# Issuing four of an image's eight key-spreading transfers from ACT instead of SP

## The reference

```python
x = x + windowed_attention(group_norm(x))         # 16 heads of 32, windows of 8 x 8, shifted
t = to_tokens(x)                                  # 256 tokens an image
h = layer_norm(t)
q, k, v = split(h @ w_qkv + b_qkv)                # 8 heads of 16
t = t + softmax(q @ k.T * scale) @ v @ w_out + b_out      # "second attention"
h = layer_norm(t)
logits = h @ router_w.T + router_b                # 8 experts, each token goes to its best 2
y = sum over 2 experts of weight * expert(h)      # silu(h1) * h2, then a second product
t = t + y
```

## Time and profile before

| | us |
|---|---|
| median of 3 runs | 778.26 |
| lowest, highest | 772.68, 778.88 |
| the profiled execution | 770.44 |
| its span from first to last instruction | 768.6 |
| share of the span that engines are busy | PE 84%, DVE 67%, ACT 66%, POOL 63% |
| mean granted clock of PE, share of full | 0.952 |

### The profile page before, as it was taken

One profiled execution on the slowest core, in us unless ns is written; L12 is line 12 of the kernel. 1 busy time (PEld: TensorE's weight loads), 2 busy tenths in 40 slices (PEclk: granted clock), 3 DMA queues, 4 the chain that ended last, 5 costly groups with the idle time before them and its releaser, 6 DMA issues. The chain is left out here.

```text
span 768.6 us, 20244 instructions
## 1 busy us (share of the span) xinstructions
PE 643.4 (84%) x7046; PEld 543.4 (71%) x7046; DVE 518.1 (67%) x1513; ACT 503.8 (66%) x1427; POOL 485.9 (63%) x556
## 2 busy tenths in 40 slices
PE   3887989999989899898998989888776699999910
PEld 2766878777778777787777878776564688888800
DVE  4666767888788878878878788884453456566524
ACT  3555788878778777888778887765551166666600
POOL 6354656665767786687867867675465436666645
PEclk9799999999999999999999999999997799999965
DMA  7102013031331303313032230312462213333246
GB/s 198 34 3 35 6 32 70 30 99 20 88 77 41 102 24 93 68 54 102 23 92 48 77 101 23 92 41 77 125 213 92 67 51 93 87 85 93 74 160 195
DMA packets 48074, 59.27 MB, mean 77 GB/s; under 512 B 10370, under 2 KB 41218, under 8 KB 47458
## 3 DMA queue, kind: packets, MB, share of 16 engines
q1 hardware_dynamic: 41846, 45.65, 22.5%
q0 software_dynamic: 4544, 9.38, 3.6%
q10 hardware_dynamic: 1584, 2.95, 1.0%
HBM read 36.00 MB, written 28.64 MB: 84 GB/s over the span
## 5 line engine op out<-in xcount | busy, mean ns | idle before, releaser
L587 POOL TENSOR_TENSOR pb<-pb,rcb 128x512 f32<-128x512 f32 x128 | 156.5, 1223 | 149.8 <-DVE rcb L873 148.5
L628 POOL DMA_INDIRECT ysl<-yo,dst x78 | 75.5, 968 | 58.4 <-DVE yo L1147 42.4
L739 ACT ACTIVATE pb<-pSB,mxb 128x256 f32<-128x256 f32 x128 | 59.5, 469 | 47.2 <-DVE mxb L973 46.6
L739 ACT ACTIVATE pb<-pSA,mxb 128x256 f32<-128x256 f32 x128 | 59.6, 475 | 41.2 <-DVE mxb L973 41.2
L1266 PE MATMUL pTB<-ident,pb 128*128 128x128 f32 x512 | 80.2, 280 | 7.2 <-ACT ptb L753 7.1
L595 POOL TENSOR_TENSOR pa<-pa,rca 128x512 f32<-128x512 f32 x64 | 67.2, 1050 | 28.5 <-DVE rca L1038 28.5
L753 ACT ACTIVATE ptb<-pTB 128x512 f32<-128x512 f32 x128 | 77.1, 602 | 2.0 <-PE pTB L1266 2.0
L523 POOL DMA_INDIRECT slots<-rec,slot x64 | 65.3, 1020 | 15.5 <-issue 14.1
L1266 PEld LDWEIGHTS pTB<-ident,pb 128*128 128x128 f32 x512 | 57.9, 142 | 11.1 <-issue 7.8
L759 ACT ACTIVATE pta<-pTA 128x512 f32<-128x512 f32 x64 | 38.6, 603 | 40.3 <-PE pTA L1358 40.1
L973 DVE TENSOR_REDUCE mxb<-pSB 128x2 f32<-128x512 f32 x64 | 43.9, 686 | 21.1 <-PE pSB L1235 21.0
(11 more groups left out here) (221 smaller groups left out, 1996.5 us busy)
## 6 DMA issues: line engine op xcount, KB each, us to landing
slots<-sel_dram SPq DMA_DIRECT2D x16, 1040.0 KB
kbd<-kst SPq DMA_DIRECT2D x128, 64.0 KB, 2.4
xt<-slots SPq DMA_DIRECT2D x39, 130.0 KB, 2.2
xch<-x_ch_dram SPq DMA_DIRECT2D x4, 512.0 KB, 7.1
xt<-x_tok_dram SPq DMA_DIRECT2D x16, 128.0 KB, 2.4
xch<-t SPq DMA_DIRECT2D x16, 128.0 KB, 2.1
fw<-f_dram SPq DMA_DIRECT2D x1, 2048.0 KB
yc<-ysl SPq DMA_DIRECT2D x8, 256.0 KB, 7.4
```

The source lines that it names most:

```text
L587: pool.tensor_tensor(pb[:, b, :, :], pb[:, b, :, :], rcb[:, b, :].unsqueeze(2).to_broadcast([128, 2, TOK]), ALU.mult).then_inc(sb_nrm, 1)
L628: pool.indirect_dma_start(ysl, bass.IndirectOffsetOnAxis(ap=dst[:, t % YB, n:n + 1], axis=0), yo[:, t % YB, n, :], None).then_inc(y_dma[t ...
L739: last = a.activation(pb[:, b, qc, :], (pSB, pSA)[n % 2][:, qc * TOK:(qc + 1) * TOK], ACT.Exp, bias=mxb[:, b, qc:qc + 1], accum_out=smb[:, ...
```

## The change

SP issues the key transfers of heads 0 to 3 only. ACT issues those of heads 4 to 7, at step 7 of the same iteration, right behind the two evictions of the queries (L710) and ahead of `t2f`. Both wait for `m_klo`, and the same semaphore counts all eight. What is moved, its bytes, its layout and all waits of PE are the same.

```diff
                     wait(sp, m_klo, M.j + 1)
                     if M.j < 2:
                         sp.wait_ge(z_k1, M.j + 1)
-                    for h in range(8):
+                    for h in range(4):
                         rows = slice(D1 * h, D1 * h + D1)
                         sp.dma_start(kbd1[M.par][rows, :, :, h % 4, :].bitcast(f32), kst1[rows, :, :, :].bitcast(f32))\
                           .then_inc(k1_dma[M.par], 16)
...
                         last.then_inc(m_qhi, 1)
+                        a.wait_ge(m_klo, M.j + 1)
+                        if M.j < 2:
+                            a.wait_ge(z_k1, M.j + 1)
+                        for h in range(4, 8):
+                            rows = slice(D1 * h, D1 * h + D1)
+                            a.dma_start(kbd1[M.par][rows, :, :, h % 4, :].bitcast(f32), kst1[rows, :, :, :].bitcast(f32))\
+                             .then_inc(k1_dma[M.par], 16)
```

## The result

The changed kernel takes 863.0 us (median of 4 runs, 861.34 to 866.76), the kernel before 776.3 in the same comparison: a ratio of 1.113 (95% interval 1.106 to 1.119). The forecast was 827 with a range of 795 to 850. The direction was right, the size was not: +87 us where I had +53. The profiled execution has a span of 861.8 us against 768.6 and a mean granted clock of 0.898 against 0.952.

A forecast was written before the change was run, and what follows sets the result against it. PE, busy 84% of the span in a stiff loop, was taken to bound the kernel. 13 images x 4.0 us plus 1 gave 53 us, so 823.4 or 831.3 by baseline; forecast the middle, 827 us, range 795 to 850.

The forecast's parts named there:

- SP loses four issues: SP's issue list: four key issues take 2.54 us instead of 5.08; SP is off the path, but the zeros go out earlier.
- ACT gains four issues: ACT ahead of `t2f`: four issues take 2.54 us, `t2f` starts 2.25 us late, PE's first scores move by 1.7 us.
- Rival A: Only ACT's stall costs, the zeros hold no keys: 13 x 1.7 + 1 = 23 us, say 798 us; chance 0.17.
- The zeros go ahead of ACT's keys: ACT's last keys land behind the zeros, so PE's first scores start 4.0 us later, bounds 1.7 and about 6.
- Behind the first scores: PE after the first scores, images 2 to 14: the 4.0 us delay passes in full, 13 x 4.0 = 52 us.
- rival C: PE's clock falls as well behind two gaps of about 2.3 us: 5.5 us an image, say 847 us; chance 0.13.
- The ends: Images without zeros beside their keys: images 0 and 1 together +1 us; image 15 taken as 0, bounds -1 and +4.
- Rival B: Zeros and ACT's keys take turns piece by piece: scores 2.3 us later an image, period 34.6, say 805 us; chance 0.13.

The follow-up runs named there:

- e1: The changed kernel, but SP waits until all eight key transfers have landed before it issues the zeros; 787.2 us, ratio 1.014.
- e6: The kernel before, with the zeros issued between the fourth and fifth key transfers and 21 filler products instead of 3; 836.9 us, ratio 1.089.
- e3: The changed kernel with 18 filler products instead of 3 ahead of the first scores; 854.9 us, ratio 1.101.
- e10: The changed kernel with ACT's four issues moved behind `t2f` and 21 filler products instead of 3; 843.4 us, ratio 1.100.
- e9: The changed kernel with the zeros written in two issues of 4 KB pieces instead of one of 33 KB pieces; 825.7 us, ratio 1.075.
- e7: The changed kernel with the second half of the zeros issued only after all eight key transfers have landed; 806.1 us, ratio 1.054.
- e2: The kernel before, all keys on SP, with the zeros issued between the fourth and fifth key transfers; 870.3 us, ratio 1.121.
- e4: The kernel before with the key transfers of heads 4 to 7 left out and PE waiting for four; 766.9 us, ratio 0.989.

## Why the prediction was right or wrong

**SP loses four issues: right.** The row of four is 2.53 us long (2.54 said), and the zeros follow 3.21 us behind the first (3.2).

**ACT gains four issues: half right.** Each issue takes 0.61 to 0.83 us, within my bounds or just above. But the earlier trace rows, where a table load stood behind an issue, was the wrong row for evictions: ACT's issues begin while evictions of its list are still running, and the stall is 1.42 us, not 2.25. PE waits 1.6 (e1) to 1.8 us (changed) for `t2f` on average, and 1.0 of it reaches the product of the values (6.17 us behind the first key issue instead of 5.19); I had 1.7. Where only this part acts, as in e1, it costs 0.5 to 0.6 us an image and not 1.7. Rival A by itself was thus much too dear (798 against e1's 787).

**The zeros go ahead of ACT's keys: the right mechanism, its term too small.** I took the scores to start 4.0 us later; they start 4.94 later (12.47 − 7.53). The working put the end of the zeros 7.1 us behind their issue and let the last 128 KB of keys follow at 100 GB/s: 8.35 us. On average the scores began 9.2 us behind the zeros' issue, in the image shown, the worst, 10.7. What was too small is the 7.1. It had been read from windows that book bytes at their start; the last rise of the zeros' semaphore comes 8.0 us behind their issue before, where few keys are in flight beside them, and 8.7 us after (8.0 to 10.2). The keys behind them add less than the 1.25 us that I had, some 0.5. The earlier trace rows had shown a longer hold, a scatter that landed 10.6 us behind the later of two zeros' issues. The bound of about 6, which I had from that row, is as far above the 4.94 as the 4.0 is below it. One reason for rival A, a DMA share of 0.65 or less, was misread too: the earlier trace rows have 0.67, and with keys and zeros in flight together the share is 1.02 from 440 to 442.

**Behind the first scores: wrong.** The step "I let the 4.0 us pass in full" had only the gap. What stands between the first scores and the next image's first key issue grew too, from 24.89 to 26.65 us, 1.8 us an image. That is the clock, rival C's mechanism, which I held for a case of 0.13 beside the forecast. It isn't beside it: gaps of the forecast's own size bring it on. In image 2 of the changed kernel PE waits 2.03 us for `t2f` and 2.10 us for the keys, where I had 2.3 and 2 to 2.5, and the clock is 0.50 from 130 to 132 and 0.53 from 136 to 138. The earlier trace rows had shown a clock of 0.58 behind a stretch with 1.5 us of gaps in four; I had expected gaps of 2.3 us and left the clock at full. e6 measures its price at 2.1 us, where I had estimated 1.5. With fillers in the gap the changed kernel too comes back to 25.1 us between the first scores and the next key issue (e3, e10).

Together: 4.94 + 1.76 = 6.7 us an image where I had 4.0. The thirteen periods behind images 2 to 14 grew by 83.8 us in the traces (73.7 + 10.1) where I had 52, so these two steps lack 32 of the 34 us by which the medians exceed the sum of 53. Rival C, at 5.5 us, 37.8 and 847 us, was the nearest of the cases.

**The ends: wrong by little.** Images 0 and 1 gave −2.4 us and not +1. Of these, 1.0 us stood already before the first key was issued (62.52 against 63.53) and is not the change's. The other 1.4 us goes with the clock as much as with the keys: nothing waits for `t2f` there and PE's wait of 1.13 us for the keys is gone, but the first scores of image 0 start 8.10 us behind the first key issue instead of 7.30, and the clock, at half from 74 to 80 before, is at half from 68 to about 71 only. Image 15 cost 3.8 us, where I took 0 with +4 as a bound: its last keys stand behind the weights as others do behind the zeros. These two nearly cancel. The 8 us at the end of the span, among the experts, belong to no step.

**Rival B and its rule.** Cut into small pieces the zeros hold less, and the keys land ahead of the zeros' end (e9): in that the traces speak for turns between the queues. That three of ACT's four transfers count 3.2 to 3.3 us does not, since they were issued ahead of the zeros or within 0.3 us of them; with no zeros near, in e1, ACT's take 2.4 to 3.6. With the zeros in 33 KB pieces the last of the four takes up to 9.7 us, the keys land with the zeros' end, and the period was 39.1, not B's 34.6. The Trainium skill (DMA: Bandwidth & Descriptors, section on queues, rings and completion order) says that an engine drains a whole packet of several descriptors before it switches to another queue. I had weighed that as if a turn were one piece. No run here shows what a packet holds; e9, with 1.8 us less hold for pieces an eighth of the size, and e7, with a hold that follows the amount, are compatible with long turns and don't prove them.

## What to carry to other kernels

Moving transfers to a second engine's queue saves issue time and gives up the order that one queue had: before it is done, look at what the shortened queue issues next, and whether that is large. Where a large transfer has slack and small ones have a reader waiting, keep it behind them, by the order in one queue or by a wait for their landing. And gaps on PE of the size seen here (two of about 2 us close together, or one of over 4) are to be priced with the clock behind them, in the likeliest case and not in a rival of its own. Last, look up whether landings in a view share one semaphore before a single transfer is called late.

## What the runs showed of the hardware

- A transfer of 64 KB in pieces of 1 KB, which lands in 2.4 us alone, took up to 9.7 us when another engine had issued a write of 1040 KB in 33 KB pieces 0.9 us before, and 6.7 us behind it in the same queue (e2). In all twelve images the last key landed 0.2 to 0.6 us behind the end of that write; with the write in 4 KB pieces it landed 1.2 to 6.8 us ahead of the end. The view has 3.2 to 3.3 us for the other three, so a median hides the one that the reader waits for.
- ACT issues ahead of its computing: its first issue began 0.76 us before the evictions of the queries that precede it in the list. What it stalls is the instruction behind the last issue.
- PE's granted clock fell to 0.50 behind gaps of 1.8 and 3.8 us, and behind gaps of 2.0 and 2.1. It stayed at 1.00 where a wait of 1.4 to 2.0 us for `t2f` was the only grown gap (e1, all twelve images), and behind one gap of 4.3 to 5.4 us it fell, but not with filler products in the gap's place; that fall cost 2.1 us an image with everything else alike (e2 against e6).
- A wait of 1.13 us for keys at image 0 stood ahead of some 6 us at half clock in the kernel before. With four transfers left out both are gone (e4), and image 1's first key issue comes 3.8 us sooner behind image 0's (26.73 against 30.53).
